# Two-layer gated cross-attention and expert kernel on one core: unrolled attention heads, identity matmuls in the second iteration, and another order inside a step

## What is computed

```python
x = x + tanh(g_xattn[0]) * L0_xattn(layernorm(x), ctx, mask, wq, bq, wk, bk, wv, bv, wo, bo)
x = x + tanh(g_ffn[0])   * L0_ffn(layernorm(x))      # GEGLU: shared expert + top-1 of 8
x = x + tanh(g_xattn[1]) * L1_xattn(layernorm(x), ctx, wq, bq, ...)
x = x + tanh(g_ffn[1])   * L1_ffn(layernorm(x))      # SiLU: shared expert + top-2 of 8
# attention: softmax(q k^T / sqrt(16)) v, per head; in layer 0 masked keys get -inf
```

## Time and profile before

| | us |
|---|---|
| Three runs of the kernel before | 1970.05, 1970.83, 1983.83 (median 1970.83) |
| The profiled execution's own time | 1979.84 |
| Its span, first to last instruction | 1978.0 |

### The profile page before, as it was taken

One profiled execution on the slowest core, in us unless ns is written; L12 is line 12 of the kernel. 1 busy time (PEld: TensorE's weight loads), 2 busy tenths in 40 slices (PEclk: granted clock), 3 DMA queues, 4 the chain that ended last, 5 costly groups with the idle time before them and its releaser, 6 DMA issues. The chain is left out here.

```text
span 1978.0 us, 26775 instructions
## 1 busy us (share of the span) xinstructions
PE 1660.8 (84%) x7489; PEld 864.0 (44%) x7490; DVE 1051.4 (53%) x2222; ACT 767.8 (39%) x1486; POOL 174.5 (9%) x243
## 2 busy tenths in 40 slices
PE   6465999969998999994499999999999999786880
PEld 3132444345665566662254444444444433543550
DVE  2565688652211122224398888787887841522334
ACT  3031577621111121120317776676776774121110
POOL 3610000000300000003000000000000000051106
PEclk9785699978999999997759998898998995697995
DMA  7934221111100987882632121111211100424114
GB/s 245 365 139 130 56 49 49 26 44 64 43 0 22 328 304 286 305 304 80 181 86 64 41 42 22 24 22 24 42 22 23 23 2 0 106 77 130 40 45 130
DMA packets 108696, 197.16 MB, mean 100 GB/s; under 512 B 8958, under 2 KB 80371, under 8 KB 108567
## 3 DMA queue, kind: packets, MB, share of 16 engines
q1 hardware_dynamic: 101633, 180.71, 29.3%
q0 software_dynamic: 4608, 12.59, 2.0%
q10 hardware_dynamic: 2326, 2.31, 0.4%
HBM read 144.69 MB, written 50.36 MB: 99 GB/s over the span
## 5 line engine op out<-in xcount | busy, mean ns | idle before, releaser
L900 DVE TENSOR_REDUCE attend_piece_max<-attend_p_bank 128x1 f32<-128x400 f32 (+3 forms) x1280 | 672.6, 590 | 155.3 <-PE attend_p_bank L793 147.5
L883 ACT ACTIVATE attend_probs<-attend_s_bank 128x512 f32<-128x512 f32 (+1 forms) x1088 | 565.5, 601 | 333.4 <-PE attend_s_bank L804 332.8
L793 PE MATMUL attend_p_bank<-attend_k_st,attend_q_st 48*128 48x400 f32 (+2 forms) x1280 | 425.8, 432 | 47.0 <-DMA attend_k_st<-ones_rows 21.1
L804 PE MATMUL attend_s_bank<-attend_q_st,attend_k_st 50*128 50x512 f32 (+2 forms) x1088 | 410.5, 493 | 32.7 <-ACT attend_probs L883 11.8
L804 PEld LDWEIGHTS attend_s_bank<-attend_q_st,attend_k_st 50*128 50x128 f32 (+2 forms) x1088 | 182.2, 198 | 385.5 <-ACT attend_probs L883 307.3
L821 PE MATMUL attend_o_bank<-attend_probs,attend_v_st 128*32 128x512 f32 (+1 forms) x2176 | 325.4, 673 | 1.4 <-ACT attend_probs L883 1.4
L793 PEld LDWEIGHTS attend_p_bank<-attend_k_st,attend_q_st 48*128 48x128 f32 (+1 forms) x1280 | 231.7, 207 | 92.4 <-issue 43.9
L1498 DVE TENSOR_TENSOR slots_hid<-slots_b_bank,slots_g_act 128x512 f32<-128x512 f32 x46 | 31.8, 692 | 159.9 <-PE slots_b_bank L1392 159.9
L1279 DVE TENSOR_TENSOR share_hid<-share_b_bank,share_g_act 128x512 f32<-128x512 f32 (+1 forms) x40 | 27.6, 691 | 149.1 <-PE share_b_bank L1160 149.1
L1468 ACT ACTIVATE slots_g_act<-slots_a_bank 128x512 f32<-128x512 f32 x46 | 27.5, 597 | 169.4 <-PE slots_a_bank L1392 169.4
L1392 PE MATMUL slots_a_bank<-slots_w_up,slots_x_t 128*128 128x512 f32 x184 | 88.1, 602 | 5.4 <-DMA slots_w_up<-in_L_ffn_W_dram 5.4
(11 more groups left out here) (208 smaller groups left out, 1368.2 us busy)
## 6 DMA issues: line engine op xcount, KB each, us to landing
slots_w_up<-in_L_ffn_W_dram SPq DMA_DIRECT2D x46, 1024.0 KB, 6.9
slots_w_dn<-in_L_ffn_W_dram SPq DMA_DIRECT2D x23, 1024.0 KB, 6.7
ctx_raw<-in_mask_BxSxS_ik_dram SPq DMA_DIRECT2D x16, 800.5 KB, 8.3
q_rows<-q_part SPq DMA_DIRECT2D x24, 512.0 KB, 4.0
attend_q_st<-q_rows SPq DMA_DIRECT2D x64, 192.0 KB, 4.5
k_rows<-ctx_k_part SPq DMA_DIRECT2D x12, 800.5 KB, 10.5
attend_k_st<-k_rows SPq DMA_DIRECT2D x32, 300.2 KB, 5.9
sorted<-keep_zeros SPq DMA_DIRECT2D x6, 1024.0 KB, 6.7
```

The costliest lines, as they stand in the source:

```text
L793: last = pe.matmul(bank[:, 0:even(kn)], q_st[rows, slot, t * P:(t + 1) * P].bitcast(F32R), k_st[rows, slot, k0:k0 + even(kn)].bitcast(F32R ...
L804: last = pe.matmul(out, k_st[rows, hs, kt * P:kt * P + kn].bitcast(F32R), q_st[rows, hs, q0:q0 + CH].bitcast(F32R), start=True, stop=not m ...
L883: act.activation(probs[0:kn, (kt + hs) % RING, q0:q0 + CH], s_bank[(NC * kt + c + hs) % RING][0:kn, :], ACT.Exp).then_inc(exp_done, 1)
L900: dve.tensor_reduce(dst, bank_of(i, n)[:, 0:kn], AX.X, ALU.max).then_inc(entry_done, 1)
```

## The change

- `Keys` gets a flag `looped`. Only the branch of layer 0 that isn't executed keeps the hardware loop; the attention of both layers as executed is written out, all sixteen heads, on every engine.
- In iteration 1, in the last two steps before scores begin (steps 2 and 3 in layer 1, 0 and 1 in layer 0), every entry is followed by `raise_clock`: two matmuls of a bf16 identity with 512 columns into `o_bank`, whose result nobody reads.
- TensorE's order inside a step becomes c0, first entry, c1, second entry, c2, all other entries (the maxima among them), c3, values, sums.
- ScalarE's copy of the output bank moves from step LATE ahead of the fourth exponential to step LATE + 1 ahead of the third.

```diff
--- before.py
+++ after.py
@@ -380,7 +380,8 @@
 class Keys:
 
 
-    def __init__(self, first, size, pieces, late, maxima_at):
+    def __init__(self, first, size, pieces, late, maxima_at, looped=False):
+        self.looped = looped
         self.first, self.S, self.pieces = first, size, pieces
         self.KT = -(-size // P)
         self.late = late
@@ -682,11 +683,12 @@
 
             def once(i):
                 body(i, i % RING, i < H, i >= 2, 1 <= i <= H)
-            for i in range(4):
+            for i in range(4 if keys.looped else H):
                 once(i)
-            with eng.Fori(4, H - RING + 1, RING) as j:
-                for u in range(RING):
-                    body(j + u, (4 + u) % RING, True, True, True)
+            if keys.looped:
+                with eng.Fori(4, H - RING + 1, RING) as j:
+                    for u in range(RING):
+                        body(j + u, (4 + u) % RING, True, True, True)
             for i in range(H, H + 2):
                 once(i)
 
@@ -744,10 +746,11 @@
                 for t, n in clears[2 * i - 2:2 * i]:
                     sp.dma_start(scratch["sorted"][l][t * P:(t + n) * P, :].rearrange("(t p) d -> p t d", p=P),
                                  const["zeros"][:, :].unsqueeze(1).to_broadcast([P, n, D])).then_inc(cleared, 16)
-            with sp.Fori(4, H - RING, RING) as j:
-                for u in range(RING):
-                    body(j + u, (4 + u) % RING, True, True, True)
-            for i in range(H - RING, H + 1):
+            if keys.looped:
+                with sp.Fori(4, H - RING, RING) as j:
+                    for u in range(RING):
+                        body(j + u, (4 + u) % RING, True, True, True)
+            for i in range(H - RING if keys.looped else 4, H + 1):
                 body(i, i % RING, True, True, True)
             sp.wait_ge(cleared, 16 * len(clears))
 
@@ -823,6 +826,12 @@
                                      start=(kt == 0), stop=(kt == KT - 1), tile_position=(0, c * VW))
                 last.then_inc(pv_done, 1)
 
+            def raise_clock():
+
+                for _ in range(2):
+                    pe.matmul(o_bank[:, :], const["ident_bf"][:, :],
+                              const["ident_bf"][:, :].unsqueeze(1).to_broadcast([P, CH // P, P]), start=True, stop=True)
+
             def body(i, slot, mx, tail, fresh):
                 if mx:
                     if isinstance(i, int) and i == 0:
@@ -834,13 +843,19 @@
                     now, before = score_step(i, slot, s, tail, fresh), pv_step(i, slot, s, tail, fresh)
                     if now and now[2] == 0:
                         wait(pe, max_in, i * (16 * PART))
-                    for chunks, first, end in (((0, 1), 0, 2), ((2,), 2, 3), ((3,), 3, None)):
-                        if chunks == (3,) and before:
-                            times_values(*before)
-                        for c in chunks if now else ():
+                    raising = isinstance(i, int) and i == 1 and LATE - 2 <= s < LATE
+                    pieces = [x for x in listed[s] if x[0] != "sums"]
+                    for c in range(NC):
+                        if now:
                             scores(*now, c)
-                        for what, at in listed[s][first:end]:
+                        for what, at in (pieces[c:c + 1], pieces[c:c + 1], pieces[c:], [])[c]:
                             entry(i, slot, what, at)
+                            if raising:
+                                raise_clock()
+                    if before:
+                        times_values(*before)
+                    for what, at in listed[s][len(pieces):]:
+                        entry(i, slot, what, at)
 
             iterations(pe, body)
 
@@ -868,7 +883,7 @@
             def body(i, slot, mx, tail, fresh):
                 for s in range(KT):
                     now = score_step(i, slot, s, tail, fresh)
-                    if not now and s == LATE and tail:
+                    if not now and s == LATE + 1 and tail:
                         copy_out(i)
                     if now:
                         h, hs, kt = now
@@ -876,7 +891,7 @@
                         if not isinstance(h, int) or KT * h + kt >= RING:
                             wait(act, pv_done, h * KT + (kt - 2))
                         for c in range(NC):
-                            if c == NC - 1 and s == LATE and tail:
+                            if c == 2 and s == LATE + 1 and tail:
                                 copy_out(i)
                             q0 = chunk_of(c)
                             wait(act, score_ready, h * (NC * KT) + (NC * kt + c + 1))
@@ -1765,7 +1780,8 @@
         }
         x_now, stats = sc.sb("x_now", [P, QT, D], F32), sc.sb("stats", [P, QT, 6], F32)
         make_constants(nc, io, const, scratch)
-        everything = Keys(0, S, PIECES, 4, (1, 2))
+        everything = Keys(0, S, PIECES, 4, (1, 2), looped=True)
+        unmasked = Keys(0, S, PIECES, 4, (1, 2))
         for l in range(2):
             if l:
                 clear_semaphores(nc)
@@ -1788,7 +1804,7 @@
                 if l == 0:
                     attend_masked(nc, const, scratch, everything, attn, row_max, mask_all, window)
                 else:
-                    attend(nc, const, scratch, l, everything, attn, row_max)
+                    attend(nc, const, scratch, l, unmasked, attn, row_max)
                 project_out(nc, const, l, attn, row_max, io["x"][0] if l == 0 else None, x_now, stats)
             with ExitStack() as part:
                 keep = Scope(nc, part, f"keep_f{l}")
```

## The result

| | before | after |
|---|---|---|
| Median of 20 runs each | 1970.74 us | 1996.87 us |
| Lowest and highest | 1950.08 to 2001.03 | 1979.35 to 2011.38 |
| Profiled execution, its span | 1979.84, 1978.0 | 1982.81, 1981.1 |

The ratio is 1.0142 (1.0114 to 1.017): 1.4% slower, where I had forecast 1967 us, no change to speak of. 1996.87 lies outside the 1950 to 1985 of the forecast itself, and inside the outer range of 1930 to 1998 only because of the room left for the rivals C and D. The profiled execution of after is the second fastest of its 20, so the two profiles differ by only 3.0 us while the medians differ by 26.1. What single profiles show is therefore read per iteration and per step, and the prices come from medians.

The account below looks back on a forecast made before the run. It took layer-1 steps to be set by TensorE waiting on ScalarE's exponential, VectorE close behind. From the median, 1970.83 - 4.1 = 1967 us (-23.2 - 2.0 - 13.5 + 34.6); own range 1950 to 1985, outer 1930 to 1998.

Parts of the forecast that it names:

- Rival C: TensorE, both layers: the identity matmuls don't raise the clock, giving 1994 us, slower; chance 0.10.
- rival D: Layer 1: the clock falls often as TensorE waits in the maxima step, 6.4 us each, four reaching 1993; chance 0.14.
- Loops gone: Layer 1: three long jump-back iterations lose 23.2 us, twelve others 2.0; bounds 15 to 26; nothing taken in layer 0.
- Identity matmuls: Iteration 1 of both layers: fillers raise TensorE's clock early, net -13.1 us in layer 0 and -0.4 in layer 1.
- Return in layer 0: Layer 0: second iteration's rest 1.7 us shorter, next three (19.08, 19.43, 14.17) become 12.50; 15.2 us gained.
- layer 1 about 4.5: Layer 1's iteration with fillers: they cost TensorE about 4.5 us if the clock rises after five, against 4.9 gained.
- The row that I had set aside: Layer 0, 209.11 to 228.54: TensorE busy 19.43 of 19.43 us at clock 0.50, speaking against a rise from fillers.
- New order: TensorE's step order, both layers: +28.7 us and +1.0 in layer 1, +4.9 in layer 0; +34.6 in all.
- e4 waits for a reduction: Layer 1, normal step: the fifth maxima product waits for VectorE to reduce the first; steps 2.80 and 2.94 us.
- maxima step: Layer 1: the last product, score chunk and values queue behind VectorE's maxima work; step 3.96 us.
- copy step: Layer 1: values reusing the output bank wait for ScalarE's copy until 2.15 instead of 1.94, +0.2 us.
- Rival B: Both layers: the order costs nothing because TensorE's bank wait is hidden; 1932 us, chance 0.29.

Follow-up runs that it names:

- unroll: The kernel before with only the heads written out, old order and old place of the copy, no identity matmuls: 1936.89 us, 0.979 of before.
- unroll_again: The unroll kernel measured a second time, unchanged: 1943.00 us, 0.9794 of before.
- unroll_order: The changed kernel without the identity matmuls (heads written out, new order, later copy): 1977.96 us, 1.001 of before, with no interval.
- ident_l0: The unroll kernel plus identity matmuls in layer 0 alone, old order: 1946.37 us, 0.9795 of before.
- entries_early: The unroll kernel with all entries ahead of score chunk 3, values still ahead of that chunk, copy unmoved: 2216.02 us; 1.0454 of before from its three shortest runs.
- both_moved: The unroll_order kernel with the output-bank copy ahead of its step's first exponential and the maxima entry behind the values: 1957.23 us, 0.989 of before.
- real_l1: The unroll kernel with one float32 matmul on 512 real weight columns after each entry concerned, layer 1 iteration 1 only: 1949.32 us, 0.9786 of before.

## Why the prediction was wrong

**Loops gone**, forecast -25.2: measured -39 (unroll), and -41 by the ratio of its repeat (0.9794). The three pauses and the low clock behind them went as worked out: iterations 2 to 15 of layer 1 take 552.0, 556.4 and 546.7 us in the profiles of before and 532.9 and 524.2 without loops, about 23 less. In layer 0, where I took nothing, iterations are 12.3 instead of 12.50, some 2 us in all. Most of the rest lies where I had not looked: behind iteration 15, in the two iterations without products. Up to the last exponential of layer 1 they take 56.5, 61.7 and 61.8 us in the three profiles of before, but 43.6 to 61.8, 49.4 in the mean, in the six profiles with written-out heads and the old order (with and without fillers); the clock makes the difference (unroll_again, then unroll_order, from the end of iteration 15 to the last exponential):

```profile
1569.30:1612.90 43.60, 36.37 (x207) 10.71 (x206) 1.48 (x6) 34.98 (x69) 0.00 (x0) 1.00 0.00 1
```

```profile
1604.30:1666.50 62.20, 55.74 (x205) 14.96 (x207) 1.48 (x6) 35.71 (x69) 0.00 (x0) 0.61 0.00 1
```

In layer 0 the same stretch takes 22.6 to 25.3 us before, 16.3 to 17.7 in four of the six and 25.2 and 25.3 in the other two. These are some 10 and 5 us in the mean, from single profiles. The mechanism in the loop was right, the term 15 us too small, and outside its bounds of 15 to 26.

**Identity matmuls**, forecast -13.5: measured +23 on the old order and, with 1996.87 beside unroll_order's 1977.96, about as much on the new one. This is the step that failed and that turned the sign: with +23 in its place my own sum gives 1967 + 36 = 2003, and with the two other terms as measured (-14 on the loops, +6 on the order) 1996. It failed twice. "Return in layer 0 ... 15.2" rested on a single profile's late rise, which two more of the same kernel did not repeat; the medians show no gain there (ident_l0 0.9795). And "layer 1 about 4.5" and "-0.4" took the rise after five entries; in four of four profiles the clock did not rise during the identity matmuls at all, and an entry with its pair cost 1.60 instead of 1.29. Iteration 1 then takes 46.44, 7.5 us more than before, near the +7.3 that I had worked out for no rise; the medians make it 20, and half of that has no place yet. Rival C, the identity matmuls don't raise the clock, holds in layer 1; in layer 0 the clock rose, for nothing. Its mechanism was priced at 1994, beside 1996.87 measured, but partly by chance: it took both layers at no gain and +13.5, and the loops' 14 us more and the order's 6 us more happened to offset most of what the fillers cost beyond that.

The row that I had set aside was right: TensorE busy 19.43 of 19.43 us at 0.50. There are stretches of 16 us in after and of 447 us in entries_early like it. By the Trainium skill (TensorE: Matmul & The Clock Gate, "What's actually happening"), under which K/N, the share of the clock that is let through, is set by how busy TensorE has been recently, both should have ended at 2.4 GHz; by "busy" as the profile's records count it, this case's traces disagree.

**New order**, forecast +34.6: measured +41 and +44. Its chain was right: e4 waits for a reduction, the old wait on the exponential is gone, maxima step 3.83 (forecast 3.96), step 0 2.66 (2.58), normal steps 2.66 to 2.82 (2.80 and 2.94). The even steps were not the long ones, because e4 and c3 start together. The copy step cost 0.47 rather than 0.2. A layer-1 iteration at full clock came out at 38.23, not 39.2, so layer 1's +28.7 was nearer 14 x 1.13 = 16; a layer-0 iteration at 13.18, not 12.85, and that against 12.3: 14 x 0.88 = +12 instead of +4.9, because its step 0 takes 4.59 (4.0). Those make 28. The remaining 13 should be the clock, for which my sum had no term. Iterations 2 to 15 of unroll_order stand 17.3 (layer 1) and 8.9 us (layer 0) above their length at full clock, those of after 12.2 and 5.0, those of unroll and unroll_again 13.5 and 4.8 (layer 1), 8.7 and 3.3 (layer 0): not clearly apart. Behind iteration 15 they are: up to the last exponential layer 1 takes 62.1 to 68.0 us in all seven profiles with the new order or the new order with copy or maxima moved, beside the 43.6 to 61.8 above, 13 us more in the mean. Why the clock falls there in the new order is not shown, and no run isolates this stretch, so this share is argued. That is rival D in kind: seven falls in layer 1 and four in layer 0, but of 1.2 to 2.8 us each, not 6.4, and in layer 1 nearly all begin in the copy step, not in the maxima step that I had blamed. Rival B, the order costs nothing, is out by more than 40 us.

What stays open: why the float32 fillers brought the rise so early and the bf16 identities did not; where half of layer 1's 20 us for the identity matmuls goes; and why both_moved, with iterations as short as unroll's, is still slower than it (0.989 beside 0.979, on another chip). Its falls in layer 1 make four iterations 1.3 us longer and one 5.1, some 10 us, but unroll's own make 13.5 and its repeat's 4.8. Behind iteration 15 it takes 62.4 us in layer 1, like the other new orders, where unroll took 61.8 and unroll_again 43.6. These are single profiles, and both_moved's is its fastest run (1942.82, median 1957.23).

The version to keep is unroll: the heads written out, the old order, no identity matmuls. It beats both kernels, in both of its tries.

## What to carry to other kernels

Before a term is built on a stretch at low clock, see whether a second profile of the same kernel has it too: the loops' pauses came back in every profile, the late rise in layer 0 not in the two others of the same kernel. In a software pipeline with rings of banks, compare orders by the chain in the special steps (the one with the copy, the one with the maxima) and move those jobs to where nothing queues behind them; moving both brought a layer-1 iteration from 38.2 to 37.0 us, though the kernel as a whole stayed 1% above the old order. Filling matmuls must be tried alone first: busy time by itself did not buy a clock rise, and even an early rise did not pay for the fillers.

## What was not expected of the hardware

- TensorE can stay at 1.2 GHz with no gap in its records: 199.63 of 200.00 us busy at 0.50 in entries_early, from a clock that had been at 1.00, in an order that differs from unroll_order only in the place of the values and of the copy. That is one profile.
- The jump back costs TensorE 2.6 to 3.3 us of pause in layer 1 (and all nine jumps in the three profiles of before), and nothing of the kind shows in layer 0, whose iterations in the loop were 0.2 us longer than straight ones.
- A filler of float32 weights on 512 columns leaves two records, 2.08 us together at half clock and 1.12 at full clock (real_l1), where a score chunk, whose operands the kernel reads as float32r, leaves one of 0.62 at half clock; a bf16 one of the identity takes 0.52 at half clock.
- Short falls of the clock in layer 1 begin nearly always at one place of an iteration, the copy step, though the iteration's longest wait is in another: six of seven in layer 1 of after, five of five in both_moved; and the five of unroll and unroll_again begin at the same change of head in the old order. What picks the iterations is open.
